# Attention with four key groups: values of two key tiles in one burst, score pairs two steps further ahead

## The reference

```python
q = _heads(hidden_states @ to_q_w)
h_txt = _sdpa(q, _heads(ehs_txt @ to_k_w), _heads(ehs_txt @ to_v_w))
h_obj = _sdpa(q, _heads(ehs_obj @ to_k_object_w), _heads(ehs_obj @ to_v_object_w))
h_oth = _sdpa(q, _heads(ehs_oth @ to_k_others_w), _heads(ehs_oth @ to_v_others_w))
h_ip = _sdpa(q, _heads(ehs_ip @ to_k_ip_w), _heads(ehs_ip @ to_v_ip_w))
out = _merge(h_txt) + _merge(h_obj) + _merge(h_oth) + _merge(h_ip)
out = out @ to_out_w + to_out_b
out = (out + residual) / RESCALE
```

## Time and profile before

| | |
|---|---|
| median of 3 runs | 2466.47 us (2464.82 to 2467.2) |
| profiled execution | 2456.19 us, span 2454.6 us |
| PE busy | 2420.3 us, 99% of the span |
| DVE busy | 1843.4 us, 75% |
| ACT busy | 1789.6 us, 73% |
| POOL busy | 412.8 us, 17% |
| granted TensorE clock | 0.999 of full |

### The profile page before, as it was taken

How to read it: one execution, slowest core, us unless ns; L and a number is a source line. 1 busy time by engine, 2 the same in 40 slices (tenths; PEclk the granted TensorE clock), 3 DMA queues, 4 the chain that set the end, 5 groups by cost and what they waited for, 6 DMA issues and landing times.

```text
span 2454.6 us, 37404 instructions
## 1 busy us (share of the span) xinstructions
PE 2420.3 (99%) x12801; PEld 1781.7 (73%) x12801; DVE 1843.4 (75%) x3288; ACT 1789.6 (73%) x3909; POOL 412.8 (17%) x567
## 2 busy tenths in 40 slices
PE   8999999999999999999999999999999999999998
PEld 7999999999999974566666666666666666666655
DVE  3457777632333478999999999999998999999983
ACT  3343433322222369999999999999999999999994
POOL 0000000000000024312223123132132132231310
PEclk9999999999999999999999999999999999999999
DMA  9645444384555666666767667677676676676761
GB/s 294 171 134 162 144 139 138 112 273 165 194 187 172 185 139 144 140 133 145 147 124 152 138 140 149 122 155 152 123 149 144 127 155 135 138 146 128 156 130 50
DMA packets 346821, 370.10 MB, mean 151 GB/s; under 512 B 94335, under 2 KB 241919, under 8 KB 346631
## 3 DMA queue, kind: packets, MB, share of 16 engines
q1 hardware_dynamic: 293232, 304.79, 54.6%
q10 hardware_dynamic: 53398, 62.93, 7.5%
HBM read 215.57 MB, written 83.89 MB: 122 GB/s over the span
## 4 chain that ended last, share of the span: by engine, by line
PE 91%; ACT 4%; DVE 1%; issue 1%; ACTq 1%; DMA 1%; SPq 0%; DVEq 0%
PE st_ps L1481 15%; PE s_ps L433 13%; PE om_ps L467 12%; PE st_ps L453 12%; PE om_ps L485 11%; PE om_ps L508 10%; PE s_ps L1533 7%; PE om_ps L1533 4%; PE s_ps L1501 3%; PE st_ps L1533 3%; ACT s_ps L604 2%; ACT probs L596 1%; ACTq L1204 1%; PE om_ps L1550 1%; PE s_ps L522 0%
## 5 line engine op out<-in xcount | busy, mean ns | idle before, releaser
L604 ACT ACTIVATE s_ps<-s_ps,negmax 128x427 f32<-128x427 f32 x1280 | 762.6, 602 | 24.2 <-DVE small L668 24.0
L659 DVE TENSOR_REDUCE negmax<-s_ps 128x2 f32<-128x854 f32 x640 | 667.3, 1043 | 77.4 <-PE s_ps L433 77.1
L596 ACT ACTIVATE probs<-st_ps 128x1024 f32<-128x1024 f32 x632 | 654.9, 1036 | 35.8 <-PE st_ps L453 31.8
L1481 PE MATMUL st_ps<-ctx_split,w_split 128*128 128x428 f32 (+2 forms) x2280 | 428.7, 348 | 8.6 <-DVE k_out L1361 8.0
L433 PE MATMUL s_ps<-kpack,qpack 96*128 96x512 f32 x1280 | 430.3, 417 | 6.5 <-ACT s_ps L604 6.1
L1481 PEld LDWEIGHTS st_ps<-ctx_split,w_split 128*128 128x128 f32 x2280 | 409.1, 188 | 26.8 <-DVE k_out L1361 9.1
L453 PE MATMUL st_ps<-qpack,kpack 104*128 104x512 f32 x1264 | 408.7, 404 | 7.5 <-ACT probs L596 6.7
L433 PEld LDWEIGHTS s_ps<-kpack,qpack 96*128 96x128 f32 x1280 | 213.1, 189 | 254.1 <-ACT s_ps L604 221.1
L401 POOL TENSOR_TENSOR small<-small,negmax 128x616 f32<-128x616 f32 x160 | 196.5, 1228 | 1098.6 <-DVE negmax L676 1098.5
L467 PE MATMUL om_ps<-probs,vt 128*32 128x512 f32 x2560 | 342.5, 607 | 2.0 <-ACT probs L596 2.0
L485 PE MATMUL om_ps<-xs,wq 128*128 128x512 f32 x1200 | 341.4, 394 | 0.4 <-DVE out L739 0.4
(11 more groups left out here) (103 smaller groups left out, 2333.0 us busy)
## 6 DMA issues: line engine op xcount, KB each, us to landing
kpack<-kT SPq DMA_DIRECT2D x240, 256.0 KB, 5.0
qpack<-q_out SPq DMA_DIRECT2D x240, 256.0 KB, 5.9
kT<-k_out ACTq DMA_DIRECT2D x160, 217.5 KB, 3.2
ctx_split_raw<-in_ctxT SPq DMA_DIRECT2D x128, 214.0 KB, 4.6
tok_pair<-in_ctxT SPq DMA_DIRECT2D x48, 512.0 KB, 4.4
xs_raw<-in_xT SPq DMA_DIRECT2D x85, 256.0 KB, 5.2
out<-in_xT SPq DMA_DIRECT2D x75, 256.0 KB, 5.8
out_yT<-out SPq DMA_DIRECT2D x75, 256.0 KB, 3.3
```

The costliest lines, as they stand in the source:

```text
L596: nc.scalar.activation(probs[:, at:at + 2, :], transposed(u, duo), ACT.Exp).then_inc(p_done, 1)
L604: last = nc.scalar.activation(s_ps[:, n % 2, z, SMALL:TOK], s_ps[:, n % 2, z, SMALL:TOK], ACT.Exp, bias=negmax[:, r, IP, j, t:t + 1], accu ...
L659: nc.vector.tensor_reduce(negmax[:, r, IP, j, t0:t0 + 2], s_ps[:, n % 2, :, SMALL:TOK], AX_X, ALU.max, negate=True).then_inc(s_max, 1)
L1481: last = nc.tensor.matmul(k_place(run, m)[:, 0:n], w[name][:, pw, q, m * P:(m + 1) * P], c[b][:, px, q, a:a + n], start=(q == 0 and z == 0 ...
```

## The change

- `values` of key tiles 0 and 1 run in one burst at step 4, those of tiles 2 and 3 in one burst at step 0 of the next slot. The ring of `probs` grows from 6 to 8.
- Slots are counted by the unit w whose transposed scores run in them. Score pair (w+2, k+2) now runs beside duo (w, k), where it was (w+2, k) beside (w, k). The work that follows a pair moves with it.
- Each step deals its query or output products to both sides of the score pair, three ahead and up to two behind, in steps 0 to 3 (output) and 4 to 7 (queries).
- DVE starts a slot with keep_queries, ahead of the pair's maximum; the heads go to step 2, add_output to step 4.
- The rings of values, maxima and sums shrink from 3 to 2. SP and POOL get new orders. An output product waits for each head by itself.

The diff, cut:

```diff
-VR = 3
+VR = 2
-PR = 6
+PR = 8
-Q_AHEAD = {5: (4, 8), 7: (11, 13)}
-Q_BEHIND = {4: (0, 4), 5: (8, 11), 7: (13, 15)}
+Q_AHEAD = {5: (2, 5), 6: (6, 9), 7: (10, 13)}
+Q_BEHIND = {4: (0, 2), 5: (5, 6), 6: (9, 10), 7: (13, 15)}
-Y_AHEAD = {1: (0, 5), 3: (10, 15)}
-Y_BEHIND = {1: (5, 10)}
+Y_SLOT = 5
+Y_AHEAD = {1: (1, 4), 2: (5, 8), 3: (10, 13)}
+Y_BEHIND = {0: (0, 1), 1: (4, 5), 2: (8, 10), 3: (13, 15)}
...
-    def duo_at(m, k):
-
-        return (m - 3, k - 6) if k >= 6 else (m - 4, k + 2)
+    def pair_at(w, k):
+
+        return (w + 2 + (k + 2) // PAIRS, (k + 2) % PAIRS)
...
+            if w > 0 and unit(w + 3):
+                pack_queries(w + 3)
+            if w > 0 and unit(w + 1):
+                load_values(w + 1)
+            if unit(w + 1):
+                pack_lse(w + 1)
+            if unit(w - Y_SLOT):
+                store_output(w - Y_SLOT)
...
-                pe.wait_ge(o_lo, w // QC * QC + QC)
+                if n % len(PASSES) == 0:
+                    pe.wait_ge(o_lo, w // QC * QC + z + 1)
...
+        def slot(w):
+            alone = w < Y_SLOT and (w + 4) % QC > 0
             for k in range(STEPS):
-                u, duo = duo_at(m, k)
-                if unit(u):
-                    scores_t(u, duo)
-                if k in (0, 2, 4) and unit(m - 4):
-                    values(m - 4, k // 2)
-                products_at(m, k, Q_AHEAD_FIRST if alone else Q_AHEAD, Y_AHEAD)
-                u, p = pair_at(m, k + 1) if k + 1 < STEPS else pair_at(m + 1, 0)
+                scores_t(w, k)
+                if k == 0 and w > 0:
+                    values(w - 1, 2)
+                    values(w - 1, 3)
+                if k == 4:
+                    values(w, 0)
+                    values(w, 1)
+                products_at(w, k, Q_AHEAD_FIRST if alone else Q_AHEAD, Y_AHEAD)
+                u, p = pair_at(w, k + 1)
                 if unit(u):
                     scores(u, p)
-                products_at(m, k, Q_BEHIND_FIRST if alone else Q_BEHIND, Y_BEHIND)
-                if k == 6 and unit(m - 4):
-                    values(m - 4, k // 2)
+                products_at(w, k, Q_BEHIND_FIRST if alone else Q_BEHIND, Y_BEHIND)
...
+        def slot(w):
+            for k in range(STEPS):
+                prob(w, k)
+                if k == 3 and unit(w + 1):
+                    logs_of(w + 1)
+                    if unit(w + 2):
+                        small_exp(w + 2, 0)
+                u, p = pair_at(w, k)
+                if unit(u):
+                    ip_sums(u, p)
+                if k == 7 and unit(w + 2):
+                    small_exp(w + 2, 1)
...
+        def slot(w):
             for k in range(STEPS):
-                if k == 0 and unit(m - 5):
-                    heads_hi(m - 5)
-                    heads_lo(m - 5)
-                row_work(m, k)
-                if k == 3 and m < LATE + 4 and unit(m - Y_LAG):
-                    add_output(m - Y_LAG)
...
+                if k == 0 and w > 0 and unit(w + 3):
+                    keep_queries(w + 3)
+                u, p = pair_at(w, k)
+                if unit(u):
+                    pair_max(u, p)
+                if k == 0:
+                    if unit(w + 1):
+                        small_sums(w + 1, 1)
+                    if w > LATE and unit(w - Y_SLOT - 1):
+                        add_output(w - Y_SLOT - 1)
+                if k == 1 and unit(w + 2):
+                    small_max(w + 2, 0)
+                if k == 2 and unit(w - 1):
+                    heads_hi(w - 1)
+                    heads_lo(w - 1)
+                if k == 4:
+                    if unit(w + 1):
+                        neg_lse(w + 1)
+                        turn_lse(w + 1)
+                    if w < LATE and unit(w - Y_SLOT):
+                        add_output(w - Y_SLOT)
+                if k == 5 and unit(w + 2):
+                    small_sums(w + 2, 0)
+                if k == 6 and unit(w + 2):
+                    small_max(w + 2, 1)
```

More of the change, by code:

```diff
@@ L157, in attention @@
     k_early = [k_first, k_second] + [below(f"kpack{r}", pack, F32R) for r in range(2, QKR - 1)]
-    v_early = [below(f"vt{r}", values_shape, F32) for r in range(VR - 1)]
+    vt = [below(f"vt{r}", values_shape, F32) for r in range(VR)]
     from_values = top
-    vt = v_early + [above(f"vt{VR - 1}", values_shape, F32)]
     kpack = k_early + [above(f"kpack{QKR - 1}", pack, F32R)]
@@ L356, in rest @@
             pack_keys(FIRST - 1)
[L357 to L359 removed]
+            for w in range(UNITS + Y_SLOT):
+                slot(w)
+                if w == 1:
                     sp.dma_start(bias[:, :], d["bias"]).then_inc(const_in, 16)
@@ L531, in output_last, with products_at @@
             last.then_inc(y_done, 1)
[L533 to L541, removed]
[L542 to L549 removed]
+        def products_at(w, k, q_at, y_at):
+            if k in y_at and unit(w - Y_SLOT):
+                output(w - Y_SLOT, range(*y_at[k]))
+            if k in q_at and unit(w + 4):
+                queries(w + 4, range(*q_at[k]))
@@ L551, in slot, with late_slot @@
                     scores(u, p)
-                products_at(m, k, Q_BEHIND_FIRST if alone else Q_BEHIND, Y_BEHIND)
-                if k == 6 and unit(m - 4):
-                    values(m - 4, k // 2)
-        def late_slot(m):
+                products_at(w, k, Q_BEHIND_FIRST if alone else Q_BEHIND, Y_BEHIND)
+        def late_slot(w):
             for k in range(STEPS):
[L559 to L569, removed]
@@ L571, in rest @@
-        def rest():
[L572 to L578, removed]
+                scores_t(w, k)
+                if k == 0:
+                    if w == LATE:
+                        values(w - 1, 2)
+                    values(w - 1, 3)
+                if k in (2, 4, 6):
+                    values(w, k // 2 - 1)
@@ L579, in rest @@
+                output(w - Y_SLOT, range(*Y_LATE[k]))
+        def rest():
+            scores(2, 2)
+            for w in range(LATE):
+                slot(w)
+            for w in range(LATE, UNITS):
+                late_slot(w)
+            output_upto_last(LAST)
+            values(UNITS - 1, 3)
             for w in range(LAST + 1, UNITS):
@@ L621, in logs_of, with first_rows @@
             nc.scalar.activation(logs[:, :, :, :], sums[:, u % VR, :, :, :], ACT.Ln).then_inc(ln_done, 1)
[L623 to L630, removed]
+        def first_rows(m, k):
             if k == 1 and unit(m - 3):
                 logs_of(m - 3)
-            u, p = pair_at(m, k)
+            u, p = first_pair(m, k)
             if unit(u):
@@ L640, in rows, with slot @@
                 small_exp(m - 2, 0)
-        def rest():
[L643 to L648, removed]
+        def slot(w):
+            for k in range(STEPS):
+                prob(w, k)
+                if k == 3 and unit(w + 1):
+                    logs_of(w + 1)
+                    if unit(w + 2):
+                        small_exp(w + 2, 0)
[4 more added lines that the diff above has]
+                    small_exp(w + 2, 1)
+        def rest():
+            small_exp(1, 1)
+            for w in range(UNITS):
+                slot(w)
+        return ActOps(first_rows, rest)
     def dve_ops(dve):
@@ L778, in rest @@
             keep_queries(FIRST - 1)
-            for m in range(FIRST, UNITS + Y_LAG + 1):
-                slot(m)
-        return DveOps(set_rows, keep_queries, rows, rest)
+            for w in range(UNITS + Y_SLOT + 1):
+                slot(w)
+        return DveOps(set_rows, keep_queries, first_rows, rest)
     return Attention(sync_ops, pool_ops, pe_ops, act_ops, dve_ops, wq, wq_raw, xs, x_raw, s_ps, st_ps, om_ps,
```

76 lines of the change are left out of this document (32 added, 44 removed).

## The result

The changed kernel takes 2505.49 us (median of 4 runs, 2500.34 to 2509.62), the kernel before 2466.47 in as many: a ratio of 1.016, 95% interval 1.0146 to 1.0174. It is slower by 39 us, outside the predicted range.

A forecast was written before the change was run, and what follows sets the result against it. It took PE to bound the kernel at 19.18 us a unit, with DVE and ACT close behind. 2,466.5 + 0.7 (71 units) - 0.6 (first five) gave 2,467 us, range 2,446 to 2,484.

The forecast's parts named there:

- Bursts: In PE's merged value bursts, a further tile costs 0.91 us instead of 1.20, saving 0.58 us a unit.
- The loop: DVE's work from keep_queries to the output, the query product behind it, then ACT back to T0: 19.19 us a unit.
- A: Likeliest case, no change: the loop through DVE sets 19.19 us a unit, 2,467 us; chance 0.38.
- B: Rival: DVE reaches the output 0.2 us sooner, units of 19.00, 2,454 us; chance 0.24.
- C: Rival: PE stays the bound at 18.60 us a unit, 2,426 us; chance 0.09.
- D: Rival: no slack at the loop's end, later exponential ends delay T7 and T0, 2,474 us, up to 2,482; chance 0.22.
- E: Rival: lse rows land late for the transposed scores, at 7.8 us 2,502 us; chance 0.07.
- Key and query packs, x loads and POOL's splits keep 5 us or more.: Transfers and POOL's splits in their new order have at least 5 us to spare, so they add nothing.
- The sum for DVE: DVE's work from keep_queries through the step 4 output adds up to 12.21 us, 12.33 with a copy's delay.
- In the first five units ... -0.6: With no output added, ACT carries the loop: 18.88 us a unit against 19.0, -0.6 us in all.
- The signs it named: Forecast is wrong if a DVE wait splits L709 to L739, or that stretch is shorter than 12.2 us.
- 1.5 us at most: In the kernel before, neither DVE nor ACT has more than 1.5 us a unit to spare.

The follow-up runs named there:

- experiment 5: Changed kernel with VectorE's add_output in step 4 put ahead of the lse instructions and turn: 2472.55 us, ratio 1.0039 to the kernel before.
- experiment 6: On top of experiment 1, the pair's maximum and copy put ahead of keep_queries in VectorE's step 0: 2454.76 us, ratio 0.9961 to the kernel before.
- experiment 1: Changed kernel, but POOL waits for the turned lse rows before splitting x chunks 2 to 4: 2467.54 us, ratio 1.0017 to the kernel before.
- experiment 7: On top of experiment 1, the five loads of wo spread over slots 0 to 3: 2462.90 us, ratio 1.0002 to the kernel before.
- experiment 12: Experiments 1, 6 and 7 with first units' query products dealt evenly and POOL's wo splits held until the lse rows are turned: 2446.85 us, ratio 0.9934.
- experiment 8: Changed kernel with the edits of experiments 1, 5, 6 and 7 together: 2462.18 us, ratio 0.999 to the kernel before.

## Why the prediction was wrong

- **Bursts, right.** A second tile costs 0.87 us, predicted 0.91.
- **The loop, right.** DVE idles ahead of L717 for PE (1.14 us, about 1 said), the first query product follows the output, and the stretch from L717 to the output's end is 12.18 us where the sum gave 12.33. The ordinary unit is 19.08, predicted 19.19: A's mechanism, halfway to B's number. B's 19.00 is what experiment 5 shows once the output has left the path, and experiment 6 shows the DVE loop itself by breaking it (18.88).
- **Rivals C, D and E did not occur.** No unit of the changed kernel with both kinds of product came near 18.60, none of the ordinary ones rose to 19.3, and from 1200 to 2390 us no transposed score waits for the lse transfers.
- **Wrong: "Key and query packs, x loads and POOL's splits keep 5 us or more."** This priced the splits at their due time alone: whether they come late for the query products, and they don't. It did not ask what they run beside. By the new order chunks 2 to 4 follow POOL's subtraction directly and are worked off from 1435.15 to 1440.96, and L697 to L702, moved to step 4, fall into just that. The sum for DVE took lse, turn and small_max at 1.85 us from the earlier trace rows, whose lse rows (1512.51 to 1513.30) fell into a gap between POOL's splits, as the lines below this list show; beside the splits it is 1.85 more. This is the failed step: a term put at nothing that was 38 us (26 by the rows, 12 by the clock behind PE's wait), and experiment 1 takes it away.
- **Wrong too: the same sentence on the query packs, and "In the first five units ... -0.6".** The loads of wo stand ahead of the second unit's pack, and PE waits 1.96 us (experiment 7 gives back 2.3). The splits of wo meet the lse rows of the third unit (experiment 12 gives back 1.6). Measured +6 us. What makes the first unit 20 to 21 long is open.
- **The signs it named were the wrong ones.** It would be wrong, it said, if a wait of DVE split the stretch from L709 to L739 or if that was shorter than 12.2 us. No wait split it, and in an ordinary unit it was 12.18, at the edge of that sign; in the units that matter it became longer, 14.0 us (1428.04 to 1442.06), which was not listed. Rival D had "with stretched DVE instructions too" at 8 us, as a small addition spread over all units. What came was one pair of engines in one unit of five.
- **What is luck.** Without the overlap (experiment 1) the ratio is 1.0017, or 2,471 us where the forecast was 2,467. That it comes so near is in part chance: the ordinary units were 0.1 us shorter than forecast (57 x 0.11 = 6 us), the first three units 6 us longer in all.
- **Two sums were slightly off.** By C's own terms 12.49 + 0.29 is 0.10 beyond 12.68, which gives 19.29 and not 19.27. The terms listed for DVE add up to some 17.5 us a unit (8 pairs, heads, queries, lse with one small_max, another small_max of 0.8, small_sums twice, output), so it had 1.7 us to spare and not 1.5 at most. Nothing hangs on either.

POOL around the lse rows, in the kernel before:

```profile
1509.59 1.29 POOL L392 TENSOR_TENSOR xs<-xs_raw,xs 128x512 fp32r<-128x512 f32 x1
1514.52 1.23 POOL L401 TENSOR_TENSOR small<-small,negmax 128x616 f32<-128x616 f32 x1 [3.64 <-DVE negmax L676]
```

On the cause, the Trainium skill (SBUF — State Buffer, section Who interferes with whom) says that VectorE and GpSimd share one pair of ports under an exclusive lock, that a VectorE instruction with two inputs in SBUF, or a copy or cast in a two-port mode, competes for it, and that tensor_reduce does not. The traces agree in which instructions were stretched: L697 and L702 (two inputs in SBUF) and the cast L700, whose mode no trace shows. Beside POOL's subtraction of 1433.71 to 1434.94 DVE's copies from PSUM took their usual time:

```profile
1434.50 0.33 DVE L676 COPY small<-s_ps 128x170 f32<-128x170 f32 x1
1434.74 0.68 DVE L730 CAST heads<-om_ps 128x512 fp32r<-128x512 f32 x1
```

A tensor_reduce that reads SBUF, L682 of the earlier trace rows, took 0.80 at 1510.47, where POOL's subtraction ran to 1510.88. The experiments show that overlap with POOL is the cause; that the ports are the reason was not measured by itself. What makes the last unit of each five 19.18 and not 19.08 stays open, as does why the clock fell behind nine of the fourteen waits and not behind the other five.

## What to carry to other kernels

When an instruction moves, look at what every other engine does at its new place, not only at what it waits for and who waits for it: a duration read from a trace holds for the neighbours it had there. An engine with 16% load can cost 38 us if its work lies beside three short instructions with an in-order queue and a full TensorE behind them, and one wait in its program takes nearly all of that back. And where two edits ease the same path (experiments 1 and 5, together in experiment 8), try them together before adding their gains, since the next resource behind it may be one that the first edit made late.

## What the runs showed of the hardware

- Three VectorE instructions on 128x64 tiles took 0.67, 0.52 and 1.37 us beside GpSimd's splits and 0.21, 0.23 and 0.27 without; the longest seen were 1.44, 1.35 and 1.67. So such a short instruction can cost about as much as the GpSimd instruction it meets: 1.37 beside a subtraction of 1.28, 1.67 beside one of 1.56 (a split of wo).
- After a wait of 1.67 us, in a stretch in which PE had otherwise been busy, the granted clock was 0.52 for 3.5 us in one unit and stayed up in another. Such a fall came behind nine of fourteen waits of 1.66 to 1.91 us and cost some 1.3 us more each time.
- Eight matmul records of a second tile in a burst add 0.87 us where a burst by itself takes 0.99 and stretches both neighbours from 0.47 to 0.57.
